# 32-head attentions: the last turn of a pair waits for one bank, additions ahead of the reciprocal, and another order of the opening

## The reference

```
queries = (x @ Wq)  -> 32 heads x 128;   keys, values = ctx @ Wk, ctx @ Wv -> 8 heads x 128
queries, keys = rope(queries), rope(keys)        # x * cos + rotate_half(x) * sin
attn = softmax(queries @ keys^T / sqrt(128) + mask)
out  = (attn @ values) -> 4096 columns;  x = layernorm(x + out @ Wo)
```

## Time and profile before

| | |
|---|---|
| median of 3 runs | 2770.38 us (2769.28 to 2778.56) |
| the profiled execution | 2777.19 us, its span 2775.9 us |
| PE busy | 2609.9 us (94%) |
| DVE busy | 1561.3 us (56%) |
| ACT busy | 1067.5 us (38%) |
| POOL busy | 711.2 us (26%) |
| chain that ended last | PE 81%, DVE 12%, ACT 4%, issue 2% |
| one group in the steady part (L744 at 289.43 to the same at 372.88) | 83.4 us |

### The profile page before, as it was taken

The page is one execution under the profiler, slowest core; times in us unless marked ns, Lnnn a source line. Parts: engine busy times, 40 slices in busy tenths (PEclk is TensorE's granted clock), DMA queues, the critical chain, the costliest instruction groups (busy, mean ns, idle before and its releaser), DMA issues.

```text
span 2775.9 us, 40831 instructions
## 1 busy us (share of the span) xinstructions
PE 2609.9 (94%) x15544; PEld 1719.2 (62%) x15544; DVE 1561.3 (56%) x2937; ACT 1067.5 (38%) x3270; POOL 711.2 (26%) x695
## 2 busy tenths in 40 slices
PE   8988999999998899889999999999998889999998
PEld 7845666666665666456666666656774454666664
DVE  3576656666546455566666666454556643344455
ACT  0014444444463355234444444523444412333331
POOL 1046334444212100362344443122211221000002
PEclk9999999999999899999999999999999999999999
DMA  8631101111001100110111110010000010000000
GB/s 182 88 129 38 33 10 38 39 39 35 20 1 38 46 2 2 33 52 6 37 38 39 38 35 4 16 69 32 2 1 28 21 63 27 15 27 1 12 1 31
DMA packets 53826, 94.91 MB, mean 34 GB/s; under 512 B 29408, under 2 KB 38560, under 8 KB 47488
## 3 DMA queue, kind: packets, MB, share of 16 engines
q1 hardware_dynamic: 53632, 92.30, 11.2%
HBM read 83.89 MB, written 8.39 MB: 33 GB/s over the span
## 4 chain that ended last, share of the span: by engine, by line
PE 81%; DVE 12%; ACT 4%; issue 2%; POOL 0%; DMA 0%; DVEq 0%; SPq 0%; POOLq 0%; ACTq 0%
PE banks L676 10%; PE banks L744 10%; PE banks L657 4%; PE banks L643 4%; PE banks L728 4%; PE banks L772 4%; PE banks L303 3%; PE banks L1897 3%; PE banks L797 3%; PE banks L1386 3%; PE banks L1949 3%; PE banks L2187 2%; PE banks L2219 2%; PE banks L1926 2%; PE banks L2252 2%
## 5 line engine op out<-in xcount | busy, mean ns | idle before, releaser
L161 POOL TENSOR_TENSOR norm_spread<-norm_mv,const 128x1 f32<-128x1 f32 x96 | 20.7, 216 | 1180.6 <-DVE norm_mv L157 1180.6
L847 ACT ACTIVATE E_x<-S_x,sm_x 128x128 f32<-128x128 f32 x512 | 199.2, 390 | 292.0 <-DVE sm_x L992 290.6
L1048 POOL TENSOR_TENSOR QT<-QT,const 128x512 f32<-128x512 f32 x128 | 171.0, 1336 | 539.6 <-DVE turned L881 539.6
L676 PE MATMUL banks<-xT,weights 128*128 128x512 f32 x512 | 236.1, 595 | 7.0 <-DVE QT L898 7.0
L956 DVE TENSOR_TENSOR x<-banks,x 128x256 f32<-128x256 f32 (+1 forms) x288 | 147.2, 511 | 129.4 <-PE banks L744 125.1
L744 PE MATMUL banks<-weights,OT 128*128 128x256 f32 x768 | 192.7, 383 | 26.6 <-DVE x L956 24.1
L744 PEld LDWEIGHTS banks<-weights,OT 128*128 128x128 f32 x768 | 140.0, 190 | 75.2 <-DVE x L956 43.9
L898 DVE TENSOR_TENSOR QT<-banks,QT 128x512 f32<-128x512 f32 x128 | 85.3, 687 | 158.0 <-ACT QT L823 146.3
L1050 POOL TENSOR_TENSOR QT<-QT,turned 128x512 f32<-128x512 f32 x128 | 167.1, 1306 | 10.0
L676 PEld LDWEIGHTS banks<-xT,weights 128*128 128x128 f32 x512 | 94.6, 190 | 116.9 <-issue 105.8
L858 ACT ACTIVATE OT<-banks 128x512 f32<-128x512 f32 x128 | 76.4, 597 | 234.4 <-PE banks L797 234.4
(11 more groups left out here) (311 smaller groups left out, 5169.6 us busy)
## 6 DMA issues: line engine op xcount, KB each, us to landing
weights<-in_L_xwq SPq DMA_DIRECT2D x16, 1024.0 KB, 4.8
weights<-in_L_xwo SPq DMA_DIRECT2D x16, 1024.0 KB, 4.8
weights<-in_L_xwk SPq DMA_DIRECT2D x16, 256.0 KB, 5.1
weights<-in_L_xwv SPq DMA_DIRECT2D x16, 256.0 KB, 2.6
weights<-in_L_ffn_W_base SPq DMA_DIRECT2D x3, 1024.0 KB, 4.9
weights<-in_L_xwq SPq DMA_DIRECT2D x4, 768.0 KB, 5.0
weights<-in_L_xwo SPq DMA_DIRECT2D x4, 768.0 KB, 5.8
xT<-in_xT SPq DMA_DIRECT2D x4, 512.0 KB, 10.0
```

Source lines behind the costliest of these rows:

```text
L676: mm = PE.matmul(to, left[:, k, head], moving, start=name in ("P1", "P2", "P4", "P5") and k == 0, stop=k == 1, skip_group_check=name in (" ...
L847: ins = AC.activation(e[:, j, :], s[:, j, :], ACT.Exp, bias=sm[:, 0, j:j + 1], scale=1.0, accum_out=sm[:, 1, j:j + 1])
L1048: PO.tensor_tensor(four(to), four(to), spread(cos128, 4), ALU.mult).then_inc(*pool_step.one())
```

## The change

Three edits in `cross`, which act in both of its stages.

1. *The last turn.* Turn 3 waits for one addition fewer (`- (turn == 3)`), and the two additions after turn 2 swap places, so that the one it waits for frees bank 6.
2. *The additions of turn 0 and 2* come ahead of the reciprocal in steps without a job 0.
3. *The opening.* The sums of xT are made in two parts, batches 4 to 6 ahead of the keys' drain and batch 7 behind it; the sine pairs of group 0 are issued later; the values of group 0 come before the keys of group 1; those keys go to banks 5 and 6 and wait for six additions in place of eight; the next users of the banks (the first query turn of group 1, the first mix) get the waits.

```diff
+                def keys_bank(g, i):
+                    return 5 + i if g == 1 else i
...
                         if g == 1:
-                            PE.wait_ge(*x_qadd(8))
+                            PE.wait_ge(*x_qadd(place_of(0, 0, "C22") + 1))
...
-                            mm = PE.matmul(psum[i][:, :], views["wk"][:, k, :], ctxT[:, k, half_of(i)], start=k == 0, stop=k == KC - 1)
+                            mm = PE.matmul(psum[keys_bank(g, i)][:, :], views["wk"][:, k, :], ctxT[:, k, half_of(i)], start=k == 0, stop=k == KC - 1)
...
-                        if n == (0 if g else 3):
-
+
+                        if g == 1 and n == 0:
+                            PE.wait_ge(*x_qadd(8))
+                        elif n == (0 if g else 3):
                             PE.wait_ge(*x_taken(NR * g + 2))
...
-                                PE.wait_ge(*xT_sums(1))
+                                PE.wait_ge(*xT_sums(2))
...
-                        if NA * q + added_at[turn]:
-                            PE.wait_ge(*x_sum(NA * q + added_at[turn]))
+
+                        free = NA * q + added_at[turn] - (turn == 3)
+                        if free:
+                            PE.wait_ge(*x_sum(free))
...
                     for i in range(2):
+                        job(0, "v", i)
+                    for i in range(2):
                         job(1, "k", i)
-                    for i in range(2):
-                        job(0, "v", i)
...
                             if u:
                                 PE.wait_ge(*x_ot(u))
+                            else:
+
+                                PE.wait_ge(*x_taken(NR + 2))
...
-                    def sums_of_xT():
-                        DV.wait_ge(*before.here(B - 1))
-                        b11, b12, b21, b22 = xT[:, 0:2, 0:HALF], xT[:, 0:2, HALF:T], xT[:, 2:4, 0:HALF], xT[:, 2:4, HALF:T]
+                    def sums_of_xT(first, end):
+
+                        DV.wait_ge(*before.here(end - 1))
+                        low, high, at = slice(first * P - HALF, end * P - HALF), slice(first * P, end * P), slice(first * P - HALF, end * P - HALF)
                         for k in range(2):
...
-                                ((lower.rearrange("p (c n) -> p c n", c=2), spread(first, 2)), (lower[:, low], second)),
+                                ((lower[:, low], second), (lower.rearrange("p (c n) -> p c n", c=2), spread(first, 2))),
...
+                    sums_of_xT(4, B - 1)
                     for kind, i in opening[:2]:
                         drain(0, kind, i)
-                    sums_of_xT()
+                    sums_of_xT(B - 1, B)
                     done = 0
-                    for kind, i in opening[2:]:
+                    for n, (kind, i) in enumerate(opening[2:]):
                         drain(0, kind, i)
-                        if kind == "q":
-                            for _ in ADDED[i % 3]:
-                                turn_queries(0, done)
-                                done += 1
+
+                        while done < (0, 0, 1, 2, 4, 8)[n]:
+                            turn_queries(0, done)
+                            done += 1
...
+                        if not jobs_at(step, 0):
+                            for j in turn_at(step, 0):
+                                add(*j)
                         if step < units:
                             DV.wait_ge(*x_exp(u + 1))
                             DV.reciprocal(sm[:, 2, :], sm[:, 1, :]).then_inc(*x_inverse.one())
-                        for j in turn_at(step, 0):
-                            add(*j)
+                        if jobs_at(step, 0):
+                            for j in turn_at(step, 0):
+                                add(*j)
```

More of the change, by code:

```diff
@@ L883, in rope_keys @@
                     def rope_keys(g, i):
-                        bank = psum[i]
+                        bank = psum[keys_bank(g, i)]
                         if i == 0 and g >= 2:
@@ L915, in drain @@
                             add_queries(g, i)
-                    def sums_of_xT():
-                        DV.wait_ge(*before.here(B - 1))
-                        b11, b12, b21, b22 = xT[:, 0:2, 0:HALF], xT[:, 0:2, HALF:T], xT[:, 2:4, 0:HALF], xT[:, 2:4, HALF:T]
+                    def sums_of_xT(first, end):
+                        DV.wait_ge(*before.here(end - 1))
+                        low, high, at = slice(first * P - HALF, end * P - HALF), slice(first * P, end * P), slice(first * P - HALF, end * P - HALF)
                         for k in range(2):
-                            then(DV.tensor_tensor(xT3[k], b22[:, k, :], b12[:, k, :], ALU.subtract))
-                            then(DV.tensor_tensor(b12[:, k, :], b12[:, k, :], b11[:, k, :], ALU.subtract))
-                            then(DV.tensor_tensor(xT2[k], b22[:, k, :], b12[:, k, :], ALU.subtract))
-                            ins = DV.tensor_tensor(xT4[k], b21[:, k, :], xT2[k], ALU.subtract)
+                            b11, b12, b21, b22 = xT[:, k, low], xT[:, k, high], xT[:, 2 + k, low], xT[:, 2 + k, high]
+                            DV.tensor_tensor(xT3[k][:, at], b22, b12, ALU.subtract)
+                            then(DV.tensor_tensor(b12, b12, b11, ALU.subtract))
+                            then(DV.tensor_tensor(xT2[k][:, at], b22, b12, ALU.subtract))
+                            ins = DV.tensor_tensor(xT4[k][:, at], b21, xT2[k][:, at], ALU.subtract)
                         ins.then_inc(*xT_sums.one())
```

## The result

The changed kernel took 2756.51 us, median of nine runs (2754.79 to 2764.03); the kernel before, run beside it, 2778.56 us, median of nine (2768.79 to 2782.16). The ratio is 0.9939, 95% interval 0.9922 to 0.9957: faster by 0.6%. The nine times of either kernel lie in two bunches (four of 2768.8 to 2770.4 and five of 2778.6 to 2782.2 before, six of 2754.8 to 2758.1 and three of 2761.8 to 2764.0 after) and the two medians fall into different ones, the upper before and the lower after, so the difference of the medians (22) says less than that of the lowest times, 14.0. The profiled execution took 2756.51 us, its span is 2755.2; before it was 2777.19 and 2775.9.

A forecast was written before the change was run, and what follows sets the result against it. TensorE was taken to set the end, stopped by a short repeating list of waits, chiefly for VectorE's additions. Turns -21.1, opening +8.8 and clock +1.2 sum to -11.1 us, giving 2759 us from a median of 2770.38; the forecast case spans 2750 to 2769.

The forecast's parts named there:

- The last turn and the additions: Output projection's turns in both stages: TensorE's waits for VectorE's additions shrink, gaining 10.55 us a stage, 21.1 us in both.
- step 7: Steps 7 of groups 1 to 5: P2 gains 1.58 us, the next group's turn 0 gains 1.16.
- step 5: Steps 5 of groups 1 to 5: P2 gains 0.38 us and about 0.15 of restart, turn 0 gains 0.31.
- the last part of the prediction: Signs in the changed profile, among them 0.2 to 0.3 us of wait for the last OT sum at turn 0.
- The second rival: Groups 1 to 5: VectorE's OT sums end no earlier and take P2's place as the wait; 2774 us, chance 0.14.
- Row sums in two parts: Stage openings: VectorE's split sums of xT delay query turn n=1 by 1.2 us in one stage, 3.1 in the other.
- All four meetings of the forecast: Opening: three VectorE row sums meet GpSimd's wq sums and one meets the key rotation, each waiting 1.0 us.
- Sine products a turn later: Group 0 of each stage: GpSimd's rotations end late, so the next group's n=1 comes 2.2 us later.
- The first rival: Openings: GpSimd and VectorE fall into step otherwise, fewer instructions meet, the opening costs nothing; 2749 us, chance 0.14.
- The clock: TensorE in the openings: low clock after idle times costs 5.7 us after the change, 4.5 before, +1.2 net.
- The rival of a low clock that stays: Longer opening idle leaves TensorE at 1.2 GHz through the first steps; from 2779 us up, chance 0.08.
- The sum: Whole kernel: -21.1 for the turns, +8.8 for the opening, +1.2 for the clock, together -11.1 us.

## Why the prediction was right, point by point

**The last turn and the additions: right, 19.8 where 21.1 stood.** The stages gained 10.17 and 9.62 of the 10.55 expected of each, and both edits without the opening 10.14 and 9.61. The working of step 7 holds row for row. VectorE in the profile after:

```profile
370.29 1.15 DVE L968 TENSOR_TENSOR x<-banks,x 128x256 f32<-128x256 f32 x2 [0.75 <-PE banks L751]
371.36 0.17 DVE L1017 RECIPROCAL sm_x<-sm_x 128x4 f32<-128x4 f32 x1
...
373.32 0.68 DVE L1003 SCALAR_TENSOR_TENSOR S_x<-banks,const 128x512 f32<-128x512 f32 x1
...
375.09 0.84 DVE L949 TENSOR_TENSOR OT<-OT 128x256 f32<-128x256 f32 x1
375.96 0.42 DVE L950 TENSOR_TENSOR weights<-OT,banks 128x256 f32<-128x256 f32 x1
376.42 0.42 DVE L951 TENSOR_TENSOR weights<-banks,weights 128x256 f32<-128x256 f32 x1
```

The reciprocal of step 7, 1.72 us late before, now costs nothing, since the additions fill the time. The second sum of OT met the rotation as forecast (0.84, where the ones around it take 0.42), and turn 0 starts 0.26 after the last sum ends. The gain of a group is 1.36, not 1.47, and not for want of the two gains forecast: step 7 gave 1.16, and step 5 gave 0.34 (from the mix to turn 0 6.93 us, 355.53 to 362.46, in place of 7.27; forecast 0.31). Its mix before is

```profile
355.60 1.02 PE L797 MATMUL banks<-PT,V 128*128 128x512 f32 x2
```

and turn 0 then came at 362.87. What the sum left out is that a turn 0 that has waited is slower itself: its eight records take 1.97 us where 1.89 were, and the mix behind them comes 0.07 later, twice in a group: 1.16 + 0.34 - 0.14 = 1.36. Of the gains of the two stages, five groups of 1.36 leave 3.4 and 2.8 for group 0 (forecast 3.2). The wait for the last sum stands in 22 places with 0.2 to 0.4 us, as the last part of the prediction had it. The second rival, that this sum takes P2's place, is out by the same rows: its waits are 6.7 us, 4.1 more than before, where P2's 24.1 went.

**Row sums in two parts: right in sign and kind, too dear.** VectorE in the opening of stage 1:

```profile
167.81 1.48 DVE L167 TENSOR_SCALAR x<-x,norm_mv,norm_rs 128x512 f32<-128x512 f32 x1 [0.44 <-POOL norm_rs L163]
169.22 1.62 DVE L933 TENSOR_TENSOR weights<-xT 128x384 f32<-128x384 f32 x1
170.76 1.61 DVE L935 TENSOR_TENSOR xT<-xT 128x384 f32<-128x384 f32 x1
172.40 1.51 DVE L936 TENSOR_TENSOR weights<-xT 128x384 f32<-128x384 f32 x1
173.95 0.56 DVE L937 TENSOR_TENSOR weights<-xT,weights 128x384 f32<-128x384 f32 x1
...
180.80 0.28 DVE L933 TENSOR_TENSOR weights<-xT 128x128 f32<-128x128 f32 x1
181.00 1.38 DVE L935 TENSOR_TENSOR xT<-xT 128x128 f32<-128x128 f32 x1
...
184.00 1.37 DVE L908 TENSOR_TENSOR QT<-banks,QT 128x512 f32<-128x512 f32 x2
```

Three instructions met GpSimd's sums of wq and took 1.51 to 1.62 in place of 0.56; one of the second part met a rotation, 1.38 in place of 0.28. All four meetings of the forecast are there. The chain from VectorE free to n=1 took 15.45 us, where the prediction's own numbers make 16.2; 0.36 of the difference are the first part (7.44 for 7.8), whose meetings cost 0.95 to 1.06 each, 0.3 the second (3.20 for 3.5). So n=1 is later by 0.5 in stage 1 (16.82 after the first keys, 16.33 before) instead of 1.25. In stage 4 it is 3.8 later (20.19 against 16.43), but there the eight records of n=3, behind an idle time of 3.95, took 5.23 us in place of 3.54, and 1.4 of these 1.7 are exposed; the chain alone, with the addition of 1147.69 done at 1148.37, gives 2.3 instead of 3.1. TensorE there (n=3 and the first four records of n=1), in stage 1 and in stage 4:

```profile
180.94 5.79 PE L679 MATMUL banks<-xT,weights 128*128 128x512 f32 x12 [0.42 <-DVE KT L899]
...
1144.63 7.11 PE L679 MATMUL banks<-xT,weights 128*128 128x512 f32 x12 [3.95 <-DVE KT L899]
```

The rule of the Trainium skill (SBUF — State Buffer, Who interferes with whom) that was weighed there holds in these rows: L935 with 128 columns starts at 181.00, 0.04 behind a rotation of 1.27 us that starts at 180.96, and ends 0.15 after it.

**Sine products a turn later: right.** Forecast and profile after, counted from n=1 at 184.74: the first scores +34.9 (219.63; forecast rotation end +34.7), S_x +39.4 (39.5), the next n=1 +43.85 (43.9).

```profile
219.63 2.01 PE L779 MATMUL banks<-KT,QT 128*128 128x128 f32 x8 [3.44 <-POOL QT L1067]
221.44 4.42 PE L679 MATMUL banks<-xT,weights 128*128 128x512 f32 x8
228.59 2.51 PE L679 MATMUL banks<-xT,weights 128*128 128x512 f32 x4 [2.74 <-DVE QT L908]
230.91 3.09 PE L679 MATMUL banks<-weights 128*128 128x512 f32 x4
```

Idle before the scores is 3.44 (3.4). Idle before n=1 is 2.7 and not 4.7, and this moves nothing: scores and query turn behind the first idle time ran partly at low clock (2.01 + 4.42 in place of 1.05 + 3.60) and used it up. In the kernel with the row sums in one piece, stage 4, they ran at full clock, and there the idle time is 4.39. The first rival, an opening for nothing, is out by the kernel that has the opening alone. What the sum hid is the size of its two halves, +6.0 and -3.8 a stage. The prediction subtracted them before looking at either, and so did not see that the good one could be had alone.

**The clock: a term of the wrong sign, inside its bounds.** Taken: 5.7 paid after, 4.5 before, +1.2. Measured: 1.7 exposed in stage 1 (the eight records from 228.59) and 1.4 in stage 4, 3.1 after, 4.5 before, -1.4. Of the four exposed idle times two were paid for, not two in three and not all four. How large the term is, is not safe: the kernel with the opening alone pays the same 3 us as the changed one, but over the eight openings of before's kind (last section) the average for two is 3.7, which makes the term -0.6, next to nothing. In stage 1 the idle time before n=3, forecast as 2.5, is 0.42, because the keys ahead of it took 8.73 us in place of 7.03, at a granted clock of 0.81 between 168 and 177, and so filled it. The rival of a low clock that stays is out: the turns behind the openings took 504.49 us in both stages.

**The sum.** Turns -19.8, chain of the opening +7.1 (0.5, 2.3, 2.2 and 2.1), clock -1.4: -14.1, where -11.1 stood. The turns (forecast 1.3 too good), the opening (1.7 too dear) and the clock (2.6 too dear) were all off by less than their bounds, and the errors partly cancel. From the median of before that the forecast started at, 2770.4, this gives 2756.3; measured 2756.5. That they agree to 0.2 us is luck: the starting point was the median of three runs, and from the median of nine, 2778.56, the same -14.1 gives 2764.5. By the medians the kernel gained 22 us, twice the 11.1 forecast; the mechanism is borne out by the ledger, not by this number.

## What to carry to other kernels

When an engine stands in front of an instruction that waits for a third engine, look what is queued behind it and who waits for that: two additions moved ahead of such a wait gave 14.9 us without a change to any semaphore, and relaxing the semaphore alone 6.1. Price the parts of a reordering one by one even where they were made as one edit; here values ahead of keys gained 3.8 us a stage and the late sines issued with them lost 6.0, and the two kernels without the late sines beat both kernels (2748.3 us, 0.9915 of before, with the row sums still in two parts, and 2751.3, 0.9919, with only the values first; by their openings 13.7 and 14.0 us below the changed kernel). All eight of their runs (2745.3 to 2752.8) are below the lowest run of the changed kernel (2754.8), and below the lowest of the kernel that keeps the late sines with the row sums in one piece, which ran beside them (2754.1). An engine off the critical path that is nearly full over a stretch, such as GpSimd's rotations in an opening, sets the order in which others should feed it: its first input early, not its consumer's first need.

## What the runs showed of the hardware that was not expected

The same code with the same idle times doesn't get the same clock. The opening of before stands in eight stretches of four profiles (before, and the three kernels with its opening): 73.46, 73.57, 73.58 and 73.58 us at full clock, 75.17 in one, and 77.72, 77.99 and 78.04 in three. In these three the keys behind the 3.70 us of idle ran partly at the low level (9.69, 9.92 and 9.89 us in place of 7.10; 8.80 in the one), and so did something earlier: the query turn n=1 behind 1.99 us of idle in the third, the first keys in the other two (8.71 and 8.73 us in place of 7.03, so that n=1 came 18.0 us after them in place of 16.3). A forecast can give such a term a spread only, and a comparison of two single profiles can be wrong by 4.5 us for each such opening.

Low clock can cost nothing where another chain is the longer one: 1.7 us more of keys in the opening of stage 1 only filled idle time. Where it was exposed it cost 1.4 to 2.8 us a stretch (1.4 the n=3 of stage 4, 2.8 the keys above).

What stays open is why unchanged code takes a different time in different executions. All of the profile but openings and turns, the same code in all twelve, takes 1585.3 to 1598.2 us. The granted clock differs too (0.96 against 1.00 in the inner windows above), and no run here was made to change that.
